# One layer of attention and a mixture of experts: the largest absolute values found on GpSimd, and the work around them put in another order

## The reference

```
x = layernorm(x + attention(x))            # x: 2 batches x 1024 tokens x 128
x = layernorm(x + mixture_of_experts(x))
attention:  q, k, v = x @ Wq, x @ Wk, x @ Wv       # 16 heads of 64
            softmax(q @ k.T / sqrt(64)) @ v, then @ Wo + bo
mixture:    an 8x8 softmax per token gives 8 logits; the best 2 of 8 experts,
            each silu(x @ a.T) * (x @ g.T) @ w2.T with 352 hidden units, weighted and summed
```

## Time and profile before

| | |
|---|---|
| median of 3 runs | 850.28 us (849.78 to 851.45) |
| the profiled execution, its own time | 851.45 us |
| its span in the trace | 849.7 us |
| PE, busy in the span | 765.0 us (90%) |
| ACT | 683.0 us (80%) |
| POOL | 677.1 us (80%) |
| DVE | 537.8 us (63%) |

### The profile page before, as it was taken

One profiled execution on the slowest core, in us unless ns is written; L12 is line 12 of the kernel. 1 busy time (PEld: TensorE's weight loads), 2 busy tenths in 40 slices (PEclk: granted clock), 3 DMA queues, 4 the chain that ended last, 5 costly groups with the idle time before them and its releaser, 6 DMA issues. The chain is left out here.

```text
span 849.7 us, 22271 instructions
## 1 busy us (share of the span) xinstructions
PE 765.0 (90%) x9183; PEld 526.3 (62%) x9183; DVE 537.8 (63%) x906; ACT 683.0 (80%) x844; POOL 677.1 (80%) x438
## 2 busy tenths in 40 slices
PE   2889999999999999999999999999989753999891
PEld 0346565656565666666666566676756443899790
DVE  5856666666766666667776566766755144865573
ACT  3799998999999898999999899989988953344352
POOL 5799888878888888889898998888999975077641
PEclk9999999999999999999999999999999975999896
DMA  5602047303030303031221213040300032113312
GB/s 176 152 2 65 16 114 112 76 5 77 4 80 2 79 2 79 9 73 32 48 64 51 65 51 96 18 110 5 79 2 5 2 88 62 43 56 93 101 42 87
DMA packets 43138, 49.30 MB, mean 58 GB/s; under 512 B 6785, under 2 KB 27655, under 8 KB 42912
## 3 DMA queue, kind: packets, MB, share of 16 engines
q1 hardware_dynamic: 39872, 43.31, 21.0%
q0 software_dynamic: 2496, 4.24, 1.5%
q10 hardware_dynamic: 672, 0.33, 0.2%
HBM read 14.28 MB, written 9.25 MB: 28 GB/s over the span
## 5 line engine op out<-in xcount | busy, mean ns | idle before, releaser
L862 POOL TENSOR_TENSOR pl<-p,ph 128x1024 f16<-128x1024 f32 x256 | 541.1, 2130 | 73.4 <-ACT ph L765 73.0
L916 DVE TENSOR_REDUCE mx<-mps 128x1 f32<-128x1024 f32 x249 | 304.1, 1221 | 131.7 <-PE mps L600 129.1
L764 ACT ACTIVATE p<-sps,escale 128x1024 f32<-128x1024 f32 x256 | 286.0, 1117 | 49.0 <-PE sps L580 43.2
L765 ACT ACTIVATE ph<-sps,escale 128x1024 f16<-128x1024 f32 x256 | 284.6, 1112 | 0.0
L675 PE MATMUL pair_bank<-v,ph 128*128 128x65 f16 x2048 | 214.7, 193 | 11.3 <-POOL pl L862 8.8
L675 PEld LDWEIGHTS pair_bank<-v,ph 128*128 128x128 f16 x2048 | 190.4, 96 | 49.0 <-POOL pl L862 17.9
L677 PE MATMUL pair_bank<-v,ph 128*128 128x64 f16 x2048 | 214.4, 195 | 0.0
L679 PE MATMUL pair_bank<-v,pl 128*128 128x65 f16 x2048 | 213.9, 192 | 0.0
L677 PEld LDWEIGHTS pair_bank<-v,ph 128*128 128x128 f16 x2048 | 190.0, 97 | 28.0
L579 PE MATMUL sps<-q_hh,k_hl 128*128 128x512 f16 x512 | 194.1, 379 | 2.3 <-ACT ph L765 1.8
L580 PE MATMUL sps<-q_lm,k_h 65*128 65x512 f16 x512 | 194.7, 380 | 0.0
(11 more groups left out here) (256 smaller groups left out, 964.9 us busy)
## 6 DMA issues: line engine op xcount, KB each, us to landing
q_hh<-hi SPq DMA_DIRECT2D x60, 128.0 KB, 2.3
q_lm<-lo SPq DMA_DIRECT2D x30, 128.0 KB, 2.4
k_h<-hi SPq DMA_DIRECT2D x30, 128.0 KB, 2.4
k_hl<-hi SPq DMA_DIRECT2D x29, 128.0 KB, 2.4
k_hl<-lo SPq DMA_DIRECT2D x29, 128.0 KB, 2.4
sorted<-pad SPq DMA_DIRECT2D x1, 2990.0 KB, 17.6
xb<-sorted SPq DMA_DIRECT2D x46, 65.0 KB, 2.0
v<-in_w1T SPq DMA_DIRECT2D x8, 352.0 KB, 3.6
```

What stands on the lines that cost most here:

```text
L764: nc.scalar.activation(p32[:, n % 4, :], sps[:, n % 2, :], ACT.Exp, bias=EXP_BIAS, scale=escale[:, 0:1])
L765: nc.scalar.activation(ph[:, n % 4, :], sps[:, n % 2, :], ACT.Exp, bias=EXP_BIAS, scale=escale[:, 0:1]).then_inc(s_exp, 1)
L862: nc.gpsimd.tensor_tensor(pl[:, n % 4, :], p32[:, n % 4, :], ph[:, n % 4, :], ALU.subtract).then_inc(s_subp, 1)
L916: nc.vector.tensor_reduce(mx[:, i // TB, i % TB:i % TB + 1], src, AX.X, ALU.max).then_inc(s_mx, 1)
```

## The change

The reduction over the partitions goes from PE and DVE to one GpSimd instruction, `partition_all_reduce`, that gives every partition the maximum of each column. With it several steps change their place: on POOL the constants and row numbers go between the `early_low_values`, and the addition of `bo` behind them; on DVE the three small factors go behind the first four pieces, and `low_inputs(1)` behind the 14 maxima; on ACT the wait for all `s_vlo`, which stood before the third `exps`, stands before the first, and a wait for `s_wvlo` is added. The buffers and semaphores of the old way are gone.

```diff
 PE:
-            pe.wait_ge(s_ident, 1)
-            pe.wait_ge(s_top, 4)
-            nc.tensor.transpose(misc[0:4, 0:P], tops[:], mem["ident"][:]).then_inc(s_topT, 1)
-            pe.wait_ge(s_high, 2)
-            pe.wait_ge(s_four, 1)
-            nc.tensor.matmul(ops[:, 0:4], ones4[:], spread_tops[:], start=True, stop=True).then_inc(s_alltop, 1)
 ACT:
             act.wait_ge(s_xlo, 2)
+            act.wait_ge(s_wvlo, 1)
+            act.wait_ge(s_vlo, PRO_V)
             act.wait_ge(s_scaled, 2)
             for n in range(LEAD_S):
-                if n == 2:
-                    act.wait_ge(s_vlo, PRO_V)
                 exps(n)
 POOL:
             pool.wait_ge(s_init, 1)
-            for k in range(FRONT_CONSTANTS):
-                front_constant(nc, pool, f, k)
-            row_ids(nc, f, 0, mem["s_ids"])
+            pool.wait_ge(s_top, 4)
+            nc.gpsimd.partition_all_reduce(alltops[:], tops[:], P, bass.bass_isa.ReduceOp.max).then_inc(s_alltop, 1)
...
             nc.gpsimd.tensor_tensor(w_lo[:, 2, :], w32[:], w_hi[:, 2, :], ALU.subtract).then_inc(s_wvlo, 1)
+            for j in range(PRO_V):
+                early_low_values(j)
+                if j < FRONT_CONSTANTS:
+                    front_constant(nc, pool, f, j)
+                if j == FRONT_CONSTANTS:
+                    row_ids(nc, f, 0, mem["s_ids"])
             pool.wait_ge(s_x, 16)
             pool.wait_ge(s_bo, 16)
             nc.gpsimd.tensor_tensor(mem["y"][:], mem["y"][:], bo[:].unsqueeze(1).broadcast_to([P, T, D]),
                                     ALU.add).then_inc(s_xbo, 1)
-            for j in range(PRO_V):
-                early_low_values(j)
 DVE:
-            nc.vector.memset(ones4[:], 1.0).then_inc(s_four, 1)
             dve.wait_ge(s_ones, 1)
-            dve.wait_ge(s_topT, 1)
-            nc.vector.tensor_reduce(highest[:], misc[0:4, 0:P], AX.X, ALU.max).then_inc(s_high, 1)
-            dve.wait_ge(s_high, 1)
-            dve.wait_ge(s_ident, 1)
-            nc.vector.tensor_scalar(spread_tops[:], mem["ident"][0:4, 0:4], highest[:, 0:1], None,
-                                    ALU.mult).then_inc(s_high, 1)
             dve.wait_ge(s_alltop, 1)
-            nc.vector.tensor_scalar(bound[:], ops[:, 0:4], 1.0 / XW_TOP, 1e-30, ALU.mult, ALU.max).then_inc(s_bound, 1)
+            nc.vector.tensor_scalar(bound[:], alltops[:], 1.0 / XW_TOP, 1e-30, ALU.mult, ALU.max).then_inc(s_bound, 1)
             dve.wait_ge(s_bound, 1)
             nc.vector.reciprocal(scales[:], bound[:]).then_inc(s_bound, 1)
             dve.wait_ge(s_bound, 2)
+            low_inputs(0)
+            low_weights(0)
+            low_weights(1)
+            for k in range(4):
+                rest_of_piece(k, k + 1, p_banks[k])
             nc.vector.tensor_scalar(qk_bound[:], bound[:, 1:3], bound[:, 0:1], 1.0 / QK_UNIT, ALU.mult,
                                     ALU.mult).then_inc(s_scaled, 1)
             nc.vector.tensor_scalar(vinv[:], bound[:, 3:4], bound[:, 0:1], 1.0 / V_UNIT, ALU.mult, ALU.mult)
             dve.wait_ge(s_scaled, 1)
             nc.vector.scalar_tensor_tensor(out=escale[:], in0=qk_bound[:, 0:1], scalar=SCALE, in1=qk_bound[:, 1:2],
                                            op0=ALU.mult, op1=ALU.mult).then_inc(s_scaled, 1)
-            low_inputs(0)
-            low_weights(0)
-            low_weights(1)
-            for k in range(4):
-                rest_of_piece(k, k + 1, p_banks[k])
             for k in range(4):
                 rest_of_piece(k, 5 + k, p1_banks[k], hi1, lo1)
-            low_inputs(1)
             for t in range(LEAD_M):
                 if t == TB:
                     negate_maxima(0, PRO_MISC - 1, None)
                 reduce_max(t)
+            low_inputs(1)
             dve.wait_ge(s_xbo, 1)
```

More of the change, by code:

```diff
@@ L446, in attention @@
         tops = sb("tops", [P, 4], F32)
-        highest = sb("highest", [4, 1], F32)
-        spread_tops = sb("spread_tops", [4, 4], F32)
-        ones4 = sb("ones4", [4, P], F32)
+        alltops = sb("alltops", [P, 4], F32)
         bound = sb("bound", [P, 4], F32)
@@ L493, in attention @@
         s_top, s_alltop, s_bound = sem("s_top"), sem("s_alltop"), sem("s_bound")
-        s_topT, s_high, s_four = sem("s_topT"), sem("s_high"), sem("s_four")
         s_wvlo, s_wv32 = sem("s_wvlo"), sem("s_wv32")
```

## The result

The changed kernel takes 861.42 us (859.55 to 862.63, 4 runs) against 850.57 us (849.78 to 851.45, 4 runs) of the kernel before: ratio 1.0126, 95% interval 1.0109 to 1.0142. It is slower, as forecast, but by 10.9 us where the sum said 6.05; 861.42 lies above the range (851.8 to 860.5). The profiled execution took 861.55 us with a span of 859.8, so its span is 10.1 us longer than the one before.

What follows compares the result with a forecast made beforehand. PE was taken to bound the main phase, so a late entry delays the end. Terms 1.85 + 0 + 3.2 + 1.0 = 6.05 us on the median of 850.28 gave 856.3 us, range 851.8 to 860.5.

Steps and rivals of the forecast that it cites:

- What bounds the kernel: Main phase: PE is the wall and enters last, so whatever delays its entry moves the end by as much.
- Term 1: Reduction at the head: taken as 3.5 us on POOL, so `bound` and the whole prologue come 1.85 us later.
- rival B: At the reduction, GpSimd's code fetch lies open: head +5.85, 860.3 us; if hidden, the forecast or A; chance 0.20.
- Term 2: POOL behind the reduction: low weights have 6.5 us to spare, cost 0; subtractions end at 49.40 plus Term 1's shift.
- Term 3: Main phase entry: first exponential 2.5 us later, PE's first weighted sum 4.05 later, 0.86 given back: +3.2 us.
- The bias branch of term 3: POOL before the first `low_parts`: bias addition of 4.50 us ends at 53.90, moving PE's first weighted sum by +4.05 us.
- The small factors: DVE in the prologue: their new place is in its 2.08 us wait before 26.56, so they cost nothing.
- The 0.86 us given back: PE at 56.45: its 0.86 us wait for a tile of values disappears because ACT is now ahead.
- Term 4: PE's gap before the third score tile grows from 1.05 to 3.3 us or more; lower clock costs 1.0 (0 to 2.9).
- A: At the head and entry: reduction costs only 0.1 to 0.5 us and the clock holds, 851.9 to 852.3 us; chance 0.17.
- C: Steps up to PE's 56.45: PE isn't the wall and makes good its loss, 848.1 us; chance 0.04.
- D: On POOL: its additions find unseen holes and the reduction costs 1.65 us, 850.3 us; chance 0.04.

Runs made afterwards that it cites:

- the all-reduce alone: The kernel before with one edit, the reduction over the partitions on GpSimd behind the constants: 854.4 us, ratio 1.004.
- the kernel with PE kept busy: The changed kernel plus 38 unread PE products between its second and third score tile: 858.69 us, ratio 1.0087 to the kernel before.
- 50 + 24 products: The kernel before plus unread PE products, 50 ahead of the transposition of `tops` and 24 before the first projection: 852.09 us, ratio 1.0012.

## Why the prediction was wrong

- **What bounds the kernel: right.** Whatever delayed the entry moved the end; the 10.31 us at the marker are 10.39 at the last `low_parts` of the main phase (685.93 and 696.32) and 10.1 at the end.
- **Term 1, the size right, the reason not shown.** `bound` moved by +1.84 (forecast +1.85). Part of the agreement is luck: `tops` was ready 0.35 us earlier in after (11.44 against 11.79), so the way from `tops` to `bound` grew by 2.19. And the reduction takes 0.39 us, not 3.5; the rest is a silent stretch of 9.31 us from 5.66 on, of which all up to 11.44 lay beside the wait for `tops`. Open behind `tops` are 3.5 us of silence. That is near rival B's hidden form, but the all-reduce alone speaks against a load of fixed length that starts when POOL comes to it. B's 860.3 us is near the result by accident, since it had the head at +5.85. That "this moves the whole prologue" holds: the +0.86 at the value stage of this pair of traces is chance, and the means over the traces differ by 2.3.
- **Term 2: right, with less to spare than thought.** POOL stood silent a second time, 7.26 us before 22.61, released by nothing but itself; the low weights ended at 27.73, where the first tile of values was asked for at 28.26. That the subtractions run without a hole held: from the first start to the last end they take 18.8 us, forecast 19.3. They end at 49.76; the forecast was 49.40 + 1.85 = 51.25, and they began 0.85 late instead of 1.85.
- **Term 3, the step that failed:** "The two other conditions are earlier: `low_inputs(1)` behind the 14 maxima ends by 45.67 + 1.20 + 1.29 = 48.2". It ended at 55.30. The 1.29 us is a row from beside a resting POOL; moved by itself the instruction keeps nearly that (1.62), moved together with the filling of POOL's queue it takes 8.15. So the entry, which was to be released by POOL at 49.45 + 1.85 = 51.30, was released by DVE at 55.45. With the instruction back in front of the maxima it is at 50.92, 0.4 from the forecast, and the time is 856.6, 0.3 from the forecast: without this step the sum, taken as a whole, held. A part of that closeness is luck, since the small factors stood 1.5 us there.
- **The bias branch of term 3.** In the changed kernel it didn't count: the bias was done at 54.21, ahead of the entry, and the first `low_parts` came 2.20 us behind the entry as in before, not 4.45. With low x back in its place it counts as forecast: bias to 55.10, first `low_parts` at 55.05.
- **The small factors,** which the prediction put at nothing: so it was in after, but one of them stood 1.1 to 2.0 us beside POOL's low weights of v in six other traces of the changed order, and 4.42 us beside the bias in one.
- **The 0.86 us given back:** about half. PE stood 0.86 us at its first transposition of the maxima in before and in the kernel with PE kept busy, but 0.40 in after (at 66.74), so 0.46 came back.
- **Term 4, right in kind, too small here:** 1.0 forecast (bounds 0 to 2.9). The distance grew by 1.79; with the 0.46 that came back the clock cost 2.25. The longer gap isn't shown to be the reason. In the traces in which the clock fell and the bias didn't hold up the first `low_parts`, the distance grew by 0.6 us behind a gap of 1.06 (50 + 24 products), by 1.5 behind 2.71, by 0.7 behind 3.43, by 1.9 behind 3.80, and by 0.6, 0.8, 1.8 and 1.9 behind gaps of 9.2 to 9.6.
- **The rivals:** A's premise (a cheap reduction) is true, its head isn't. C and D are refuted: there was no further idle of PE to absorb a late start.

In numbers, forecast and measured:

| | forecast | measured |
|---|---|---|
| entry | +4.37 | +8.52 |
| bias ahead of the first `low_parts` (4.05 - 2.52) | +1.53 | 0 |
| given back at the transposition | -0.86 | -0.46 |
| clock | +1.0 | +2.25 |
| sum | 6.04 | 10.31 |

The entry alone is 4.15 us off, nearly the whole miss of 4.3. The other three are off by -1.53, +0.40 and +1.25 and nearly cancel.

The parts don't add as single edits would have it: +0.21, +0.34, +0.40 and +0.40% sum to 1.35% beside 1.26%, but with stalls in different places.

## What to carry to other kernels

Before an instruction is moved on DVE or POOL, look at what the other of the two does at its new place: a duration from a row is good only for that row's neighbours, and with two operands from the on-chip memory on both sides one of them stands, here for one instruction of the other or for as long as its queue ran. A new kind of GpSimd instruction is to be priced with the silence before it and the silence behind it, not by its own duration. One trace on either side is not enough for differences of a microsecond: the first value tile moved by 0.86 us in the pair and by 2.3 in the means. Where PE has a gap before a phase that it bounds, see what the granted clock is when it resumes.

## What was unexpected of the hardware

- Two-operand instructions of DVE and POOL exclude each other. DVE's 1.29 us became 8.15, a 128x1 instruction's 0.16 became 4.42, a one-operand reduction stayed at 1.20; where DVE got in, POOL's 1.13 became 2.11.
- The all-reduce of 128x4 takes 0.39 us but brings two silent stretches of POOL, 9.31 us before and 7.26 behind. The Trainium skill (GPSIMD Engine Reference, 2.1 Instruction dispatch) has about 6 us for the load of a new function's code, with no instruction shown. The traces agree that there is a silence and show it longer, on the way back as well, and beginning ahead of the instruction's own wait. What it is made of they don't show: 1.75 us later at the instruction, POOL started it only 0.3 us later.
- PE's products went from 0.63 to 0.38 us between 2.5 and 5.9 us after its first projection, in kernels alike up to there and with the granted clock shown as 1.00 throughout (14 to 30 us in before and after); products without a reader, fitted into its idle time at the start, made the kernel before 0.40% faster.
